# Attention in a two-layer transformer kernel: the weights' transposes two query blocks at once, the residual sum on ScalarE and GpSimd, and 135 blocks of rows in the second experts

## The reference

```
q, k = rope(xn @ Wq.T), rope(xn @ Wk.T);  v = xn @ Wv.T
out     = softmax(causal(q @ k.T * scale)) @ v
geo_out = softmax(causal(qp[..., :, None] * kp[..., None, :])) @ v
out = out + head_scales * (geo_out - out)
h = h + out @ Wo.T
x = x + ga * h
```

```
h = val * silu(gate)            # of xn @ w_up[e].T
y = h @ w_down[e].T
out = sum over the token's 2 experts of y * c, plus the skip
```

## Time and profile before

| | |
|---|---|
| median of 3 runs (lowest, highest) | 2249.42 us (2247.61, 2254.61) |
| the profiled execution, and its span | 2250.27 us, 2248.3 us |
| busy over the span: PE, DVE, ACT, POOL | 77%, 74%, 59%, 52% |
| mean granted clock of TensorE | 0.865 |
| attention phase | about 99 to 668 us |
| busy from 400 to 500 us: PE, DVE, ACT, POOL | 88.6, 98.8, 69.3, 71.5 us |
| second experts' scatters | 1912 to 2198 us |

### The profile page before, as it was taken

The page is one execution under the profiler, slowest core; times in us unless marked ns, Lnnn a source line. Parts: engine busy times, 40 slices in busy tenths (PEclk is TensorE's granted clock), DMA queues, the critical chain, the costliest instruction groups (busy, mean ns, idle before and its releaser), DMA issues. The chain is left out here.

```text
span 2248.3 us, 44945 instructions
## 1 busy us (share of the span) xinstructions
PE 1736.2 (77%) x13802; PEld 1370.2 (61%) x13802; DVE 1664.0 (74%) x5243; ACT 1333.8 (59%) x3237; POOL 1163.7 (52%) x1241
## 2 busy tenths in 40 slices
PE   5688888889975655839994777777777651999994
PEld 5577777777753442426663555555566551999993
DVE  7599999999975882438986899999755342555554
ACT  4477767666743993218782788888444331555551
POOL 3267767777740004842414788888724455444440
PEclk8699999999986757969996999999865555999997
DMA  3000000000003112341200000000130011222218
GB/s 112 13 1 2 2 2 2 2 2 2 2 26 141 36 48 54 47 115 57 66 10 0 1 1 1 1 1 1 66 116 31 32 40 58 69 66 64 66 53 230
DMA packets 103547, 92.21 MB, mean 41 GB/s; under 512 B 11729, under 2 KB 93905, under 8 KB 102609
## 3 DMA queue, kind: packets, MB, share of 16 engines
q1 hardware_dynamic: 80272, 62.84, 9.1%
q0 software_dynamic: 14592, 22.30, 3.8%
q10 hardware_dynamic: 8448, 4.20, 0.6%
HBM read 46.33 MB, written 42.98 MB: 40 GB/s over the span
## 5 line engine op out<-in xcount | busy, mean ns | idle before, releaser
L2251 POOL TENSOR_TENSOR delta_A<-delta_A,delta_sW 128x256 f32<-128x256 f32 x256 | 193.8, 757 | 78.6 <-ACT delta_sW L2098 52.2
L2021 PE MATMUL delta_u<-delta_m,tables_sb 128*128 128x256 f32 x512 | 166.4, 407 | 82.0 <-DVE delta_m L2171 82.0
L643 ACT ACTIVATE attn_p_att<-attn_score,attn_mx 128x224 f32<-128x224 f32 (+7 forms) x512 | 145.7, 396 | 139.3 <-DVE attn_mx L724 139.3
L2871 POOL DMA_INDIRECT choice_rows<-ffn_y,ffn_xg x136 | 130.0, 956 | 172.4 <-DVE ffn_y L2978 168.1
L629 ACT ACTIVATE attn_p_geo<-attn_kp_wide,attn_geo_cols 128x32 f32<-128x32 f32 (+6 forms) x448 | 179.4, 498 | 0.0
L572 PE MATMUL attn_score<-attn_k,attn_q_diag 128*128 128x64 f32 (+5 forms) x1024 | 177.8, 317 | 0.0
L2098 ACT ACTIVATE delta_sW<-delta_W,tables_sb 128x256 f32<-128x256 f32 x256 | 126.6, 506 | 79.5 <-DVE delta_W L2193 75.6
L2021 PEld LDWEIGHTS delta_u<-delta_m,tables_sb 128*128 128x128 f32 x512 | 87.2, 190 | 132.3 <-DVE delta_m L2171 125.6
L2017 PE MATMUL delta_u<-delta_v_own,tables_sb 128*128 128x256 f32 x512 | 153.6, 382 | 8.7 <-DVE xnT L2158 8.7
L572 PEld LDWEIGHTS attn_score<-attn_k,attn_q_diag 128*128 128x128 f32 x1024 | 149.5, 193 | 7.3
L2828 POOL DMA_INDIRECT rows<-mix_rows,mix_slot x128 | 123.8, 967 | 55.9 <-issue 52.2
(11 more groups left out here) (399 smaller groups left out, 5011.6 us busy)
## 6 DMA issues: line engine op xcount, KB each, us to landing
ffn_xg<-rows SPq DMA_DIRECT2D x136, 66.0 KB
acc<-route_zero SPq DMA_DIRECT2D x10, 832.0 KB
comb_rows<-choice_rows SPq DMA_DIRECT2D x32, 256.0 KB
rows<-route_rows SPq DMA_DIRECT2D x8, 640.0 KB, 3.4
load_rows<-in_x SPq DMA_DIRECT2D x16, 256.0 KB, 4.9
bT<-acc SPq DMA_DIRECT2D x16, 256.0 KB, 4.1
qT<-acc SPq DMA_DIRECT2D x16, 256.0 KB, 4.8
x_kept<-xT SPq DMA_DIRECT2D x16, 256.0 KB, 2.1
```

Of the source, the lines that this page charges most:

```text
L643: last = nc.scalar.activation(p_att[:, gr, ROW_OFF[n]:ROW_OFF[n + 1]], score[at][:, c:c + SLOT * (n + 1)], ACT.Exp, bias=mx[:, gr, n:n + 1])
L2021: nc.tensor.matmul(corrections(h, pp % 2), g.t("same_head"), m1[:, h].rearrange("p t d b -> p (t d b)"), start=False, stop=True).then_inc( ...
L2251: nc.gpsimd.tensor_tensor(A[:, t % 8], A[:, (t - 1) % 8], sW[:, t % RING], ALU.add).then_inc(k.A, 1)
L2871: nc.gpsimd.indirect_dma_start(g.choice_rows, bass.IndirectOffsetOnAxis(xg[:, n % RING, D:D + 1].bitcast(U32), 0), y[:, n % RING, :], None ...
```

## The change

In three parts:

1. `p_att` is laid out by pairs of query blocks (`PAIR_OFF`): both blocks of a pair get as many key blocks as the second of them needs, so that the even block has one more, which is cleared once and never written. `turn_att` then turns a pair in one instruction: 4 instructions of 4, 8, 12 and 16 blocks instead of 8 of 1 to 8.
2. `add` leaves VectorE. ScalarE's new `gate(b)` copies `v_out` with the gate as scale into a new SBUF tensor, `gated`; it stands at the end of the iteration, behind `front(b+1)`. GpSimd's `add(b)` sums `gated` into `x`; it stands in `geo`, between the two products (L853, L855) and the operations on `geo_own`. `front_v` on TensorE waits for the gate instead of the add. The last two adds stand around the last `combine`.
3. `TILES1` is 135.

```
-TILES1 = K1 * N // 128 + E1
+TILES1 = K1 * N // 128 + E1 - 1
...
-ROW_OFF = [SLOT * n * (n + 1) // 2 for n in range(KB + 1)]
+PAIR_OFF = [SLOT * (2 * (n // 2) * (n // 2 + 1) + n % 2 * (2 * (n // 2) + 2)) for n in range(KB + 1)]
...
-        p_att = s.sb("p_att", [128, GROUPS, ROW_OFF[KB]])
+        p_att = s.sb("p_att", [128, GROUPS, PAIR_OFF[KB]])
+        gated = s.sb("gated", [128, T])
...  (TensorE, front_v)
-                    pe.wait_ge(k.x_done, b - 1)
+                    pe.wait_ge(k.gated, b - 1)
...  (ScalarE, att_exps; new gate)
-   nc.scalar.activation(p_att[:, gr, ROW_OFF[n]:ROW_OFF[n + 1]],
+   nc.scalar.activation(p_att[:, gr, PAIR_OFF[n]:PAIR_OFF[n] + SLOT * (n + 1)],
+            def gate(b):
+                act.wait_ge(k.out_made, b + 1)
+                act.wait_ge(k.x_done, b)
+                nc.scalar.activation(gated[:, :], v_out_ps[:, T:2 * T], ACT.Copy, scale=g.mod[:, 0, 2, bass.ds(b, 1)])\
+                    .then_inc(k.gated, 1)
...  (end of ScalarE's iteration, and behind the loop)
+                if b > 0:
+                    gate(b - 1)
+            gate(B - 1)
...  (VectorE, before the loop; turn_att)
+            nc.vector.memset(p_att[:, :, :], 0.0).then_inc(k.cleared, 1)
-                for n in range(KB):
-                    last = nc.vector.transpose(by_key(0, gr)[:, 0:n + 1, SLOT * n:SLOT * n + SLOT],
-                                               p_att[:, gr, ROW_OFF[n]:ROW_OFF[n + 1]].rearrange("p (j i) -> p j i", i=SLOT))
+                for n in range(0, KB, 2):
+                    last = nc.vector.transpose(by_key(0, gr)[:, 0:n + 2, SLOT * n:SLOT * n + 2 * SLOT]
+                                               .rearrange("p j (n i) -> p n j i", n=2),
+                                               p_att[:, gr, PAIR_OFF[n]:PAIR_OFF[n + 2]].rearrange("p (n j i) -> p n j i", n=2, i=SLOT))
...  (VectorE: add and its two calls removed)
-                dve.wait_ge(k.out_made, b + 1)
-                nc.vector.scalar_tensor_tensor(x, v_out_ps[:, T:2 * T], g.mod[:, 0, 2, bass.ds(b, 1)], x, ALU.mult, ALU.add)\
-                    .then_inc(k.x_done, 1)
...  (GpSimd: new add; its place in geo, behind the two products; around the last combine)
+            def add(b):
+                pool.wait_ge(k.gated, b + 1)
+                x = g.xT[:, tokens(b)]
+                nc.gpsimd.tensor_tensor(x, x, gated[:, :], ALU.add).then_inc(k.x_done, 1)
+                if b > 1:
+                    add(b - 2)
+            add(B - 2)
             combine(B - 1)
+            add(B - 1)
```

More of the change, by code:

```diff
@@ L507, in attention_phase @@
                    " rows_copied less_qp kp_copied ran_max ran_min ga_made gb_made less_max geo_cols geo_own"
-                   " recip coef combined out_turned summed out_made x_done")
+                   " recip coef combined out_turned summed out_made gated x_done")
         by_bank = [s.sems("scored max_read att_exp", n) for n in range(BANKS)]
@@ L523, in _ @@
             pe.wait_ge(k.w_in, 64)
-            pe.wait_ge(k.cleared, 2)
+            pe.wait_ge(k.cleared, 3)
             pe.wait_ge(k.ones, PER)
@@ L621, in _ @@
         def _(act):
-            act.wait_ge(k.cleared, 2)
+            act.wait_ge(k.cleared, 3)
             def geo_exps(b, par, gr):
@@ L642, in att_exps @@
                         if at == bank:
-                            last = nc.scalar.activation(p_att[:, gr, ROW_OFF[n]:ROW_OFF[n + 1]],
+                            last = nc.scalar.activation(p_att[:, gr, PAIR_OFF[n]:PAIR_OFF[n] + SLOT * (n + 1)],
                                                         score[at][:, c:c + SLOT * (n + 1)], ACT.Exp, bias=mx[:, gr, n:n + 1])
@@ L674, in _ @@
             nc.vector.memset(mx[:, :, :], 0.0).then_inc(k.cleared, 1)
-            dve.wait_ge(k.cleared, 2)
+            nc.vector.memset(p_att[:, :, :], 0.0).then_inc(k.cleared, 1)
+            dve.wait_ge(k.cleared, 3)
             for h in range(PER):
@@ L768, in turn_mixed @@
                                     aoT[:, :, :, :, :].rearrange("p o n g d -> p (o n g d)")).then_inc(k.summed, 1)
-            def add(b):
-                dve.wait_ge(k.out_made, b + 1)
-                x = g.xT[:, tokens(b)]
-                nc.vector.scalar_tensor_tensor(x, v_out_ps[:, T:2 * T], g.mod[:, 0, 2, bass.ds(b, 1)], x, ALU.mult, ALU.add)\
-                    .then_inc(k.x_done, 1)
             front_qk(0)
@@ L793, in _ @@
                 turn_att(b, 1)
-                if b > 0:
-                    add(b - 1)
                 if b + 1 < B:
@@ L803, in _ @@
             turn_mixed(B - 1)
-            add(B - 1)
         @block.gpsimd
```

## The result

| | before | changed |
|---|---|---|
| median of 13 runs (lowest, highest), us | 2249.96 (2246.71, 2263.8) | 2242.08 (2233.36, 2244.97) |
| profiled execution, span, us | 2250.27, 2248.3 | 2244.97, 2242.6 |

A forecast was written before the change was run, and what follows sets the result against it. VectorE was taken to bound attention, 32 iterations of 17.10 us. The terms -10.8 - 5.0 + 8.4 + 0.8 + 0.7 - 2.1 = -8.0 us took the profiled 2250.27 to 2242.3, the median to 2241.4; range 2232 to 2249.

The forecast's parts named there:

- The add off VectorE, 0.36 us: Attention, VectorE's queue: the add's departure frees 0.36 us in each of 30 iterations, 10.8 us gained.
- Transposes, 0.08 a group: Attention, VectorE: four wide transposes for eight save 0.08 us in 63 groups, 5.0 us gained; bounds 3.8 and 6.9.
- the rival of slow transposes: VectorE's transposes: one more dimension in the write slows them, at double time 84 us lost, 2325; chance 0.06.
- The collision, 0.28 us: Attention: GpSimd's add holds up VectorE's minimum of run_max and run_min by 0.28 us in 30 iterations, 8.4 us lost.
- The rival of a dearer collision: Attention: GpSimd's add takes 1.07 us or waits for the gate, VectorE's minimum waits 0.62, total 2251.6; chance 0.18.
- The no-collision rival: Attention: VectorE's minimum slips ahead of GpSimd's add or isn't held up, giving back 8.4 us, total 2233.0; chance 0.20.
- The hold for the whole instruction: VectorE's minimum beside GpSimd's add: by the skill's page it would wait 0.39 us, 11.7 us lost in place of 8.4.
- Gate, GpSimd's queue: ScalarE's 0.44 us gate hides in 3.57 us of idle, GpSimd's 0.72 us add in 1.62: no cost in either queue.
- TensorE's drops of the clock, 0.8 us in all: Attention from about 500 us: in five iterations at the lower clock, less TensorE slack loses 0.16 us each, 0.8 us.
- Start, nothing: Start of attention: clearing p_att takes 2.3 us on VectorE, hidden under TensorE's wait for the weights, so no cost.
- End, 0.7 us: End of attention: copy, hand-over and GpSimd's add replace one VectorE instruction of 0.48 us, 0.7 us lost.
- 135 blocks, 2.1 us: Second experts: one block less saves one rhythm of the scatters, 2.12 us apart, 2.1 us gained.

The follow-up runs named there:

- e3: The changed kernel with GpSimd's add in front of the two products, one batch later; ratio to the kernel before 0.9917, period 16.50 us.
- e2: The kernel before with only the add moved to ScalarE and GpSimd, eight transposes, 136 blocks; ratio to the kernel before 0.9978, period 16.98 us.
- e5: The changed kernel with GpSimd's add behind the three operations on geo_own; ratio to the kernel before 0.9892, period 16.50 us.
- e4: The changed kernel with GpSimd's add made 512 wide, adding zeros in the second half; ratio to the kernel before 1.0026, period 17.32 us.
- e10: The kernel before with 135 blocks alone; one execution of 2198.5 us beside 2195.49 of the kernel before, period 17.10 us.

## Why the prediction was right, step by step

- **The add off VectorE, 0.36 us:** right; in e3, free of the collision, the period is 17.10 - 0.60 = 16.50, which is 0.36 + 0.22 within 0.02. Net of the collision the move gives 0.12 an iteration (e2) where I had 0.08: some 1 us more over 30.
- **Transposes, 0.08 a group:** a little low. They save 0.11, the value by the slope and the upper part of my bound. The 512-wide one fits the line of the smaller ones (663 ns in the mean, 661 by the slope); the extra jump in the write costs 12 ns on the 128-wide one (274 against 262) and 1 to 2 ns on the others, and the rival of slow transposes is out.
- **The collision, 0.28 us:** right in size and place, and in each of the 22 of 30 iterations that don't follow a drop of TensorE's clock (below). e3, e5 and e4 show the mechanism by taking it away twice and stretching it, e2 and e4 by the constant distance of the two ends. The rival of a dearer collision needed a longer add, and e4 shows what that gives. The no-collision rival is refuted by the 0.68 us record.
- **The hold for the whole instruction (the Trainium skill, "SBUF — State Buffer", section "SBUF: two separate sides"), against the rows' 0.12 us less:** the rows win. The minimum ends 0.28 behind the add's end and needs 0.41, so its hold ends 0.13 us before the end of GpSimd's record.
- **Gate, GpSimd's queue:** hidden, as covered. The gate takes 0.56, not 0.44, and 2.7 us of idle are left behind it.
- **TensorE's drops of the clock, 0.8 us in all:** mis-sized, and read at the wrong place. The rows at 510 us that I took for those at the lower clock are at the full one: in before the granted clock is 0.50 from 499.9 to 503.3 us, and the wait comes some 7 us later. The changed kernel's profile has eight such drops of 3.4 us in attention, not five. The first lasts from 258.7 to 262.1 us. Two stretches of the changed kernel, in it and behind it (from:to and length, busy time of PE, PEld, DVE, ACT and POOL with instructions, granted clock, DMA share, GB/s):

```profile
259.00:262.00 3.00, 3.00 (x10) 1.83 (x13) 3.00 (x10) 2.11 (x8) 3.00 (x4) 0.50 0.00 0
262.00:270.00 8.00, 8.00 (x153) 7.01 (x146) 7.00 (x19) 5.22 (x17) 4.29 (x5) 1.00 0.01 2
```

  At a clock of 0.50 TensorE's product of k with the directions (L553) takes 1.91 us instead of 1.03, and at the full clock again the second `weigh` starts at 267.62, 1.6 us behind its place, and uses up TensorE's slack. VectorE there:

```profile
267.18 1.09 DVE L735 TENSOR_REDUCE attn_mx<-attn_score 128x2 f32<-128x384 f32 x3 [0.30 <-PE attn_score L573]
268.18 0.41 DVE L722 TENSOR_TENSOR attn_geo_rows<-attn_run_max,attn_run_min 128x256 f32<-128x256 f32 x1
...
270.01 1.31 DVE L765 STREAM_TRANSPOSE attn_oT<-attn_out 128x512 f32<-128x512 f32 x2 [0.58 <-PE attn_out L587]
...
271.75 0.19 DVE L772 TENSOR_TENSOR attn_coef<-attn_coef,attn_share 128x32 f32<-128x32 f32 x1
```

  VectorE waits 0.30 for scores and 0.58 for the outputs. The minimum starts 0.39 late and turn_out 0.65 later still; but, being late, the minimum meets no add (0.41) and the product no geo_own (0.19), which gives back 0.27 and 0.52. That leaves 0.25, and the starts of turn_out say the same: 252.47, 270.01 and 286.29 are two periods of 33.82 together, where 33.56 is the rule. The later drops cost 0.28 to 0.30 each, all eight some 2.3 us (the eighth, at the phase's end, is taken as the others). I had 0.16 each and five of them; before has five and pays 0.01 each.
- **Start, nothing:** wrong by 0.4 us. The clearing of p_att takes 2.19 us, but starts 0.48 us late:

```profile
100.08 0.91 DVE L683 MEMSET attn_v_diag<- 128x1024 f32 x1 [4.16 <-PEq L140]
...
101.50 2.19 DVE L685 MEMSET attn_p_att<- 128x2560 f32 x1 [0.48 <-issue]
103.76 0.49 DVE L689 MEMSET attn_v_diag<- 32x16 f32 x4
...
106.69 0.69 DVE L698 TENSOR_TENSOR attn_tq<-attn_q_rows,tables_sb 128x512 f32<-128x512 f32 x1 [2.05 <-PE attn_q_rows L529]
```

  The fills end at 104.25, 4.17 behind the first clearing's start instead of 1.49, and tq starts 6.61 behind it instead of 6.17 (105.10 in before). TensorE's first product now waits for the fills and not for the weights: it starts 4.43 behind the first clearing's start instead of 3.95. I had given this term 0.2 us of cover and had not counted the 0.48 of idle.
- **End, 0.7 us:** right. The chain at the end of attention in the changed kernel:

```profile
658.03 0.71 DVE L779 STREAM_TRANSPOSE attn_ao<-attn_aoT 128x512 f32<-128x512 f32 x1 [1.31 <-POOL attn_aoT L820]
...
660.97 0.47 ACT L663 ACTIVATE attn_gated<-attn_v_out,mod 128x256 f32<-128x256 f32 x1 [8.69 <-PE attn_v_out L596]
661.52 0.72 POOL L856 TENSOR_TENSOR xT<-xT,attn_gated 128x256 f32<-128x256 f32 x1 [3.53 <-ACT attn_gated L663]
```

  From the start of the last mixed transpose to the end of the sum it is 4.21 us, against 3.42 before.
- **135 blocks, 2.1 us:** right, by the scatters' first and last starts.

Summed over the profiled pair: attention from tq to the last sum 562.45 and 555.55 us (-6.9, the period's 0.31 x 31 less drops and the end), the start +0.4, the experts -2.1, so -8.6 in what the change touches, where I had -8.0; the load phase before it was 1.2 us longer and the rest 1.7 us longer, neither touched by the change. That the profiled pair differs by 5.3 and the medians by 7.9 is in line with a spread of 11.6 us among the changed kernel's runs; its profiled run was the slowest of 13. That the medians came out within 0.7 us of the forecast is partly luck of errors that cancel: 0.03 us too little on 63 groups of transposes (-1.9) and 0.03 to 0.04 on 30 adds (-1) against drops (+1.5), start (+0.4) and end (+0.1).

## What to carry to other kernels

Work moved from VectorE to GpSimd is not free when a VectorE instruction with two SBUF inputs, or a fast copy from SBUF to SBUF, starts while the GpSimd instruction runs: it waits until about 0.13 us before that one's end and then does all its work. Look in the timeline for records far above their own minimum (0.74 against 0.19) and place GpSimd's instructions where VectorE is in PSUM reductions or transposes: here the same add costs 0.28 us an iteration in one slot of its queue and nothing in two others, of which the later one spends TensorE's slack. After each microsecond gained on the bound engine, read the next engine's slack again; two moves later TensorE's chain was the bound, and exchanging two steps on a third engine freed it.

## What the hardware showed that I had not expected

- A one-input copy of 256 elements from SBUF to SBUF is held as well (281 ns alone, 553 beside GpSimd's add).
- GpSimd's add over 512 elements took 1.27 us where its other 512-wide products take 1.08; in all 31 iterations, whether the minimum meets it early or late; why stays open.
- The number of drops to the lower clock in attention is not set by the code alone: five in before and eight in e10, whose attention is the same. The changed kernel has eight; in the five runs with a period of 16.50 us or less there are none between 150 and 600 us, in one profile each. What sets it was not tried, and neither was whether fewer drops belong to the gain of those runs. At the full clock the periods repeat to about 0.01 us.
- The same code, the kernel before, runs at 2250 us on one chip and at 2196 to 2202 on others, and nearly all of the difference lies in one phase: from its first to its last instruction the mixing phase takes 278.0 us in the profile of before and 228.9 in e2, whose code there is the same; the spans are 2248.3 and 2193.0. The stretch of the mixing phase in each (busy time as above), VectorE 128 us busy in both:

```profile
1617.60:1895.60 278.00, 162.81 (x816) 139.25 (x816) 128.41 (x524) 99.73 (x229) 132.96 (x157) 0.57 0.19 67
```

```profile
1610.10:1839.00 228.90, 146.31 (x816) 127.98 (x816) 128.08 (x524) 98.74 (x229) 134.60 (x157) 0.62 0.23 81
```

  TensorE was granted less there too (0.57 against 0.62). Why stays open. This is why ratios, and not times, are compared across chips.
